# Relative attention on one core: transfers after the products, scores one tile ahead, band one quad earlier

## What is computed

```python
idx = jnp.arange(s)
dist = jnp.clip(idx[None, :] - idx[:, None], -R, R) + R
pe_k = rel_emb_k[dist]
pe_v = rel_emb_v[dist]
score = jnp.einsum('bhqd,bhkd->bhqk', q, k) + jnp.einsum('bhqd,qkd->bhqk', q, pe_k)
attn = jax.nn.softmax(score, axis=-1)
ctx = jnp.einsum('bhqk,bhkd->bhqd', attn, v) + jnp.einsum('bhqk,qkd->bhqd', attn, pe_v)
```

## Time and profile before

| what | us |
|---|---|
| median of 3 runs (2241.8 to 2245.21) | 2243.42 |
| the profiled execution: its time | 2241.7 |
| the profiled execution: span of its records | 2240.0 |
| first to last max (L1196) | 1244.1 to 1976.1 |
| TensorE busy in the span | 1690.1 (75%) |
| VectorE busy | 1069.3 (48%) |
| ScalarE busy | 873.6 (39%) |
| GpSimd busy | 488.9 (22%) |

### The profile page before, as it was taken

One profiled execution on the slowest core, in us unless ns is written; L12 is line 12 of the kernel. 1 busy time (PEld: TensorE's weight loads), 2 busy tenths in 40 slices (PEclk: granted clock), 3 DMA queues, 4 the chain that ended last, 5 costly groups with the idle time before them and its releaser, 6 DMA issues. The chain is left out here.

```text
span 2240.0 us, 35061 instructions
## 1 busy us (share of the span) xinstructions
PE 1690.1 (75%) x12902; PEld 1140.2 (51%) x12902; DVE 1069.3 (48%) x2108; ACT 873.6 (39%) x1448; POOL 488.9 (22%) x717
## 2 busy tenths in 40 slices
PE   2668888865519999996284678687867878887798
PEld 1323333244417777774132556565755756754554
DVE  5556666435401111111462656575755757732454
ACT  1115555641201111110240656575755757733221
POOL 0201111100040000001341335354443545410000
PEclk9859999977559999998585899898988989975798
DMA  2351211000232223210245565757667575510111
GB/s 63 96 141 19 37 19 19 1 6 0 102 127 73 73 73 105 73 51 31 70 169 71 149 158 157 156 154 166 156 158 158 159 155 155 158 54 14 39 56 56
DMA packets 206912, 206.07 MB, mean 92 GB/s; under 512 B 19734, under 2 KB 185502, under 8 KB 206758
## 3 DMA queue, kind: packets, MB, share of 16 engines
q1 hardware_dynamic: 202279, 190.41, 32.6%
q0 software_dynamic: 4480, 13.64, 1.7%
HBM read 121.61 MB, written 82.18 MB: 91 GB/s over the span
## 5 line engine op out<-in xcount | busy, mean ns | idle before, releaser
L1196 DVE CUSTOM_DVE_ANT_0 prob<-ps,dev 128x1024 f32<-128x1024 f32 x256 | 312.2, 1220 | 203.9 <-PE ps L1020 176.0
L1029 PE MATMUL ps<-cst,prob 128*128 128x128 f32 x2048 | 293.9, 280 | 16.0 <-issue 9.3
L1094 ACT ACTIVATE prob<-prob,nmax 128x1024 f32<-128x1024 f32 x256 | 295.0, 1152 | 21.4 <-DVE nmax L1196 21.0
L1029 PEld LDWEIGHTS ps<-cst,prob 128*128 128x128 f32 x2048 | 241.7, 144 | 58.9 <-issue 39.8
L1658 PE MATMUL ps<-xeT,w 128*128 128x320 f32 x896 | 244.3, 435 | 1.5 <-ACT xeT L1683 1.5
L763 ACT ACTIVATE pT<-ps 128x512 f32<-128x512 f32 (+3 forms) x384 | 168.2, 494 | 176.3 <-PE ps L723 174.6
L800 DVE TENSOR_REDUCE nmax<-ps 128x1 f32<-128x128 f32 (+7 forms) x256 | 184.3, 753 | 102.2 <-PE ps L704 100.5
L1658 PEld LDWEIGHTS ps<-xeT,w 128*128 128x128 f32 x896 | 171.2, 191 | 72.7 <-issue 3.1
L1020 PE MATMUL ps<-ks,qs 96*128 96x512 bf16 (+4 forms) x768 | 161.0, 320 | 33.2 <-DVE nmax L1196 21.3
L1203 DVE COPY probT<-ps 128x512 f32<-128x512 f32 x256 | 175.8, 687 | 17.9 <-PE ps L1029 17.8
L1101 ACT ACTIVATE probT<-ps 128x512 f32<-128x512 f32 x256 | 152.6, 596 | 72.3 <-PE ps L1029 71.5
(11 more groups left out here) (304 smaller groups left out, 2294.9 us busy)
## 6 DMA issues: line engine op xcount, KB each, us to landing
dev<-skew_u SPq DMA_DIRECT2D x128, 256.0 KB, 3.8
skew_p<-prob SPq DMA_DIRECT2D x128, 256.0 KB, 3.7
w<-in_L_ffn_w SPq DMA_DIRECT2D x24, 896.0 KB, 6.3
skew_u<-cst SPq DMA_DIRECT2D x64, 256.0 KB, 3.7
wr<-skew_p SPq DMA_DIRECT2D x128, 128.0 KB, 2.2
qs<-qd SPq DMA_DIRECT2D x96, 128.0 KB, 4.2
ks<-kd SPq DMA_DIRECT2D x48, 256.0 KB, 12.1
qd<-parts SPq DMA_DIRECT2D x48, 128.0 KB, 1.8
```

Source lines behind the costliest of these rows:

```text
L1029: last = nc.tensor.transpose(ps[:, ring_bank(job), kb * P:(kb + 1) * P], prob_tile(t, (4 * h + kb) * P, (4 * h + kb + 1) * P), k.c("ident"))
L1094: nc.scalar.activation(prob_tile(t, 0, S), prob_tile(t, 0, S), ACT.Exp, bias=nmax[:, t % 4:t % 4 + 1], scale=-1.0).then_inc(s_exp, 1)
L1196: nc.vector.tensor_tensor_reduce(out=prob_tile(t, 0, S), in0=scores, in1=dev_tile(t), scale=-1.0, scalar=3.0e38, op0=ALU.add, op1=ALU.min, ...
```

## The change

Four things are reordered; no instruction is added or taken away.

- In `order`, value goes ahead of turn within step 4k, and relative is done for quad k+3, with relative(2) ahead of the loop.
- TensorE alone does row(t+1) where the list has row(t), with row(0) and row(1) at the start. VectorE and ScalarE keep their places for row(t).
- SyncE: within a step, dev and skew_p come first, then wr of the same pair (step s now has wr of pair s-1), then the band, then a load.
- GpSimd: at even t the zone sum of a pair comes first; band_of(t//4+3) follows at t%4 == 2, with band_of(2) ahead of the loop.

```diff
@@ steps() @@
                 if t < TILES:
                     yield "row", t
+                if t % 4 == 0 and 0 <= t // 4 - 2 < QUADS:
+                    yield "value", t // 4 - 2
                 if 0 <= t - 3 < TILES:
                     yield "turn", t - 3, 0
                     yield "turn", t - 3, 1
-                if t % 4 == 0 and t // 4 + 2 < QUADS:
-                    yield "relative", t // 4 + 2
-                if t % 4 == 0 and 0 <= t // 4 - 2 < QUADS:
-                    yield "value", t // 4 - 2
+                if t % 4 == 0 and t // 4 + 3 < QUADS:
+                    yield "relative", t // 4 + 3
...
-        order = [("relative", 0), ("relative", 1)] + list(steps())
+        order = [("relative", 0), ("relative", 1), ("relative", 2)] + list(steps())
@@ SyncE @@
-                for step in range(-3, PAIRS + 2):
-                    if 0 <= step - 2 < PAIRS:
-                        m = step - 2
-                        sp.wait_ge(s_po[m % 3], 16 * (m // 3 + 1))
-                        if m >= 4:
-                            sp.wait_ge(s_w, m // 2 - 1)
-                        sp.dma_start(wr[:, m // 2 % 2, m % 2 * 2:m % 2 * 2 + 2, :], skewed(skew_p, m % 4 * 2, 2)).then_inc(s_wr[m % 4], 16)
-                    if step % 2 and (step + 3) // 2 < QUADS:
-                        n = (step + 3) // 2
...
+                for step in range(-4, PAIRS + 1):
                     if 0 <= step + 2 < PAIRS:
...
                         sp.dma_start(skew_p[i:i + 2].rearrange("h p w -> p h w"),
                                      bass.AP(at.tensor, at.offset, [list(at.ap[0]), [PITCH, 2], [1, 2 * P]])).then_inc(s_po[m % 3], 16)
+                        sp.wait_ge(s_po[m % 3], 16 * (m // 3 + 1))
+                        if m >= 4:
+                            sp.wait_ge(s_w, m // 2 - 1)
+                        sp.dma_start(wr[:, m // 2 % 2, m % 2 * 2:m % 2 * 2 + 2, :], skewed(skew_p, m % 4 * 2, 2)).then_inc(s_wr[m % 4], 16)
+                    if step % 2 == 0 and (step + 4) // 2 < QUADS:
+                        n = (step + 4) // 2
+                        sp.wait_ge(s_band, n + 1)
+                        for m in (2 * n - 4, 2 * n - 3):
+                            if m >= 0:
+                                sp.wait_ge(s_dev[m % 3], 16 * (m // 3 + 1))
+                        sp.dma_start(skewed(skew_u, n % 2 * HQ, HQ), band[:, n % 2, :, :]).then_inc(s_bo[n % 2], 16)
                     if step > 0 and step % 16 == 0 and step // 16 + 1 < GROUPS:
@@ TensorE @@
+                def row(t):
+                    r, a, n = t % HQ, t // HQ % KB, t // HQ // KB
+                    if r == 0 and a == 0:
+                        pe.wait_ge(s_lk[n % 2], LD * (n // 2 + 1))
+                    if t >= 2:
+                        pe.wait_ge(s_max, t - 1)
...
                 for step in order:
+                    if step == ("row", 0):
+                        row(0)
                     if step[0] == "row":
...
+                        if step[1] + 1 < TILES:
+                            row(step[1] + 1)
@@ GpSimd @@
                 band_of(1)
+                band_of(2)
                 for t in range(0, TILES + 8, 2):
-                    if t % 4 == 0 and t // 4 + 2 < QUADS:
-                        band_of(t // 4 + 2)
                     if 0 <= t // 2 - 2 < PAIRS:
                         zone_sum(t // 2 - 2)
+                    if t % 4 == 2 and t // 4 + 3 < QUADS:
+                        band_of(t // 4 + 3)
```

More of the change, by code:

```diff
@@ L1007, in near @@
                     last.then_inc(s_rel, 1)
+                def row(t):
[4 more added lines that the diff above has]
+                        pe.wait_ge(s_max, t - 1)
+                    edges = sorted({0, 512, a * P + R, S})
+                    for lo, hi in zip(edges, edges[1:]):
+                        last = nc.tensor.matmul(ps[:, 2 * (t % 2) + lo // 512, lo % 512:lo % 512 + hi - lo],
+                                                qs[:, n % 2, r, a * P:(a + 1) * P], ks[:, n % 2, r, int(lo >= a * P + R), lo:hi],
+                                                start=True, stop=True)
+                    last.then_inc(s_row, 1)
                 job = 0
                 for step in order:
+                    if step == ("row", 0):
+                        row(0)
                     if step[0] == "row":
[L1012 to L1023, removed]
+                        if step[1] + 1 < TILES:
+                            row(step[1] + 1)
                     elif step[0] == "turn":
```

## The result

The changed kernel takes **2268.2 us** (median of four runs, 2267.9 to 2268.8) against 2244.0 before (four runs as well): a ratio of 1.0100, interval 1.0083 to 1.0118, some 24 us slower. The direction was forecast, the size (+6) was not. The profiled execution took 2268.46 us with a span of 2266.8, 26.8 more than the span before.

A forecast was written before the change was run, and what follows sets the result against it. It took a TensorE-VectorE chain (10.09 us a quad) and six load stalls to bound the kernel. Ordinary quads +6.5, heads quads -5.0, loads +3.6 and start +0.6 made +5.7, say +6: 2249 us beside the median, range 2231 to 2266.

The forecast's parts named there:

- What bounds the kernel now: Ordinary quads: a TensorE-VectorE chain of 10.09 us, SyncE's queue needing 9.63; plus a 13.0 us stall at six head loads.
- Part 1: SyncE's order: at a load the stall moves from reduce to max; skew_p(s) lands 1.6 us later (bounds 0.5 and 3.1).
- Part 4: Quad after the stall: 12.3 us from skew_p(s)'s landing against 13.29 before; with the shift, each load costs +0.6 us.
- Part 2: TensorE's order: ordinary quads 10.22 us against 10.09, idle time moving from max to copy; heads quads win 0.55.
- Part 3: Band and relative a quad earlier: ScalarE's copy has 1.2 us slack; nothing taken in ordinary quads, bounds 0 to 0.3 us.
- the first rival: ScalarE's wait for the band bites: late wr cost 0.3 us in each of 50 ordinary quads, 2264 us; chance 0.15.
- The rival on the other side: Load stall shrinks: landing shift 0, quad after it about 10.6 us, -2.7 for each of 6, 2229 us; chance 0.20.
- The reorder changes nothing: Hand-overs at their low bound give ordinary quads of 10.0 us, or halfway a sum of 0, 2243 us; chance 0.25.

The follow-up runs named there:

- e7: Kernel before with VectorE's reduce ahead of max(4k+1) instead of behind copy(4k-2): 2251.7 us, 1.0029 of before.
- e2: Changed kernel with relative and band_of back where the kernel before has them: 2266.7 us, 1.0087 of before.
- e4: Kernel before with SyncE's new loop alone (load behind wr and the band): 2259.3 us, 1.0073 of before.
- e6: Kernel before with value ahead of turn(4k-3) alone, row not ahead: 0.9993 of before.
- e13: Kernel before with the head load waiting for skew_p(s-1) to land, still issued ahead of wr(s-1): 2259.6 us, 1.0058 of before.
- e9: Kernel before with both TensorE orders alone (row one tile ahead, value ahead of turn(4k-3)): 1.0018 of before.
- e3: Changed kernel with the head load put back between skew_p(s-1) and wr(s-1): 2257.3 us, 1.0048 of before.
- e11: Kernel before with dev issued from ScalarE's queue instead of SyncE's, loads left in place: 2254.2 us, 1.0031 of before.
- e12: Kernel before with dev and the six later loads from ScalarE's queue, one load transfer every second tile: 2193.3 us, 0.9750 of before.
- e8: Kernel before with the six later head loads issued by ScalarE, one transfer a tile over twelve tiles: 2227.7 us, 0.9907 of before.

## Why the prediction was wrong in size

- **What bounds the kernel now**: the first step that failed. I read that SyncE's loop needs 9.63 us a quad against 10.09 and took 0.46 us as slack, so that the engines' chain sets the pace. 9.63 us was one quad with landings of 3.06 and 4.08; in e7, where it hardly waits for an engine, the queue needs 10.3 on average. A load holds the queue and the engines for about 13 us, and what lateness SyncE then has against the engines it wins back slowly or, in e2, e4 and e6, not at all before the next load. The trace of the kernel before shows how little slack there was: SyncE waited for an exponential only 17 us in 600. I then treated the load stall and the quads between as separate sums; e2, e4 and e6 show that they share one account.
- **Part 1, the load's shift**: 1.6 us forecast, 2.65 measured (26.35 - 23.70), inside the bounds 0.5 to 3.1, mis-sized by two thirds. The load is issued 4.21 us after skew_p(s-1) on average (4.41 in the timeline above) instead of 0.47, 3.7 us later; about 1 us comes back, as it takes 22.1 us from the load's issue to skew_p's landing instead of 23.2. That this is the 384 KB of wr and band, now ahead of the load instead of behind it, fits e13, where they are behind it and it takes 23.5. I had counted only the time in which no data moves. e13 shows that the whole wait counts: its load goes out 3.29 us after skew_p(s-1), 2.8 later than before, and skew_p(s) lands 3.07 us later. The Trainium skill's rule on the fixed cost of a DMA (DMA: Bandwidth & Descriptors; it stands in the section Anatomy of one DMA — SWDGE (gpsimd) path, not in the one that the prediction names, and is given for transfers that GpSimd issues) spoke in the right direction; its 2 us falls short of the 3.07 that e13 adds by waiting for one landing.
- **Part 4, the cost of a load**: +0.6 forecast, +0.67 measured (35.46 - 34.79), and that is luck. It is made of +2.65 (the landing), -0.90 (11.85 us after it where it was 12.75; 12.3 was forecast) and -1.07 (the engines come later, 2.73 for 1.66), a term that the sum doesn't have. Without the band's waits it is +2.6 (e2 against before), with the load moved alone +2.8 (e4).
- **Part 2, the ordinary quad**: chain right, link for link; 10.22 forecast, 10.34 measured. Row to near is 0.54 for 0.45, turn to copy 1.13 and 1.11 for 1.08. +7.9 us against +6.5, though there are 42 ordinary quads outside the load pairs and not 50, and the forecast should have read +5.5. Heads quads won 0.12 instead of 0.42 each. But e9 shows that of this only some 0.2% reach the end.
- **Part 3, ScalarE's wait for the band**: 0 taken, 0.3 us a quad as the upper bound (+15, the first rival, at 0.15); measured 14.6 us, in seven quads of up to 4.7 and not evenly. The slack of 1.2 us was counted from an average landing; around the quad shown, three even pairs in a row took 6.13, 5.26 and 5.03 us to land, where 4.1 is usual. And a stall of TensorE is paid again where its clock has dropped, as in the quad shown. The rival had the right place and by luck the price (it priced 50 even quads, and seven uneven ones paid), and still isn't the cause: with the wait undone (e2) the time stays within 2 us.
- **The rival on the other side**, a shorter stall at the load, needed a landing shift below 0.3 us; it is 2.65. "The reorder changes nothing" is out too.

What is left, by the ratios: the moved load is 0.52 to 0.73% (changed against e3, e2 against e9, e4 against before), both TensorE orders 0.14 to 0.18% (e2 against e4, e9 against before), the early band 0.13 to 0.30% (changed against e2, e3 against e9). In microseconds that is 12 to 16, 3 to 4 and 3 to 7, where the sum had +3.6 for the loads, +1.5 for the quads and +0.6 for the band: the moved load is the term that was mis-sized most. That each path of differences adds up to 1.0% is no proof, it does so by construction. Each ratio is known to 0.15 to 0.29% either way and a difference of two to 0.2 to 0.35%, so only the moved load is clear of the noise on all three of its comparisons. The two small parts are at its edge: each is clear on one comparison (0.18 for the orders, 0.30 for the early band) and not on the other. Why some landings of skew_p take over 5 us in a row was not tried and stays open.

## To carry to other kernels

Before costing quads, ask which engine or queue hardly ever waits for the others. A queue that stops for each landing can be such a one even where a single quad shows slack, and then a gain elsewhere is given back at the next place where it is late: time a quad of that queue over many quads, not one. Put a large transfer into such a queue before a wait for a landing, not behind it (0.5 to 0.7% here); better, give it another queue in small pieces (0.9% here). Where two stalls share one pacer, taking one away may show only at the other: e6 and e2 won nothing, e11 alone lost 0.3%, and e12, with the loads moved as well, won 2.5%.

## What the runs showed of the hardware

With dev and the loads issued from ScalarE, SyncE's transfers no longer stand behind the large ones: the stage moves 165 GB/s at a DMA share of 0.65 (158 at 0.63 with one queue), and from the first to the last of the 64 reduces it takes 674 us where one queue took 725 (e12 against before). But dev then stands behind the load's pieces, and a landing of skew_p still slows beside them (up to 6.4 us on average in e8). In e11, where the load stayed whole on SyncE's queue and only dev was issued from ScalarE, ScalarE was stopped up to 16.7 us at a time. A wait for one landing ahead of a 2.3 MB load cost 3.1 us in the time to the landing behind it (e13), although no byte more was moved.
